# Two orders in the first graph layer: where the scalar engine takes the fourth bank, and where the matrix engine turns the rows

## What is computed

```python
for l in range(3):
    si = x @ attn_w[l, :d]
    sj = x @ attn_w[l, d:]
    scores = si[:, :, None] + sj[:, None, :] + attn_b[l]
    scores = jnp.where(scores >= 0, scores, 0.2 * scores)
    scores = jnp.where(mask, scores, -jnp.inf)
    attn = jax.nn.softmax(scores, axis=-1)
    agg = jnp.einsum('bij,bjd->bid', attn, x)
    h = layernorm(x + agg, g1[l], beta1[l])
    ff = jax.nn.gelu(h @ W1[l] + b1[l], approximate=False) @ W2[l] + b2[l]
    x = layernorm(h + ff, g2[l], beta2[l])
```

## Time and profile before

| | |
|---|---|
| median of three runs | 2901.18 us (2900.43 to 2902.38) |
| profiled execution | 2900.89 us, its span 2899.1 us |
| PE busy over the span | 2633.2 us (91%) |
| DVE | 2045.2 us (71%) |
| ACT | 1928.1 us (67%) |
| POOL | 1674.6 us (58%) |
| first graph layer | about 1304 to 1819 us |
| second and third graph layer | about 1819 to 2780 us |

### The profile page before, as it was taken

How to read it: one execution, slowest core, us unless ns; L and a number is a source line. 1 busy time by engine, 2 the same in 40 slices (tenths; PEclk the granted TensorE clock), 3 DMA queues, 4 the chain that set the end, 5 groups by cost and what they waited for, 6 DMA issues and landing times. The chain is left out here.

```text
span 2899.1 us, 117800 instructions
## 1 busy us (share of the span) xinstructions
PE 2633.2 (91%) x44450; PEld 2409.1 (83%) x44608; DVE 2045.2 (71%) x6167; ACT 1928.1 (67%) x5044; POOL 1674.6 (58%) x2677
## 2 busy tenths in 40 slices
PE   7999999978888888859999999999999999999956
PEld 5777777767777777758999998999999999999945
DVE  6787888844444444448888887777777788888868
ACT  4666666644444444437888887788888778888734
POOL 6777777710000000017888886666666678888845
PEclk9999999999999999979999999999999999999979
DMA  3111111000000000020000001100000100000002
GB/s 90 39 40 39 36 36 36 22 9 13 13 13 13 13 13 13 13 76 25 25 24 25 25 25 39 50 9 9 9 9 9 28 32 9 9 9 9 8 12 105
DMA packets 110837, 74.60 MB, mean 26 GB/s; under 512 B 51504, under 2 KB 109360, under 8 KB 110512
## 3 DMA queue, kind: packets, MB, share of 16 engines
q1 hardware_dynamic: 96800, 61.03, 7.3%
q10 hardware_dynamic: 13968, 12.72, 1.5%
HBM read 51.68 MB, written 22.02 MB: 25 GB/s over the span
## 5 line engine op out<-in xcount | busy, mean ns | idle before, releaser
L1638 PE MATMUL g_H<-g_hT_upper,g_w_upper 128*128 128x256 f32 x1536 | 461.4, 300 | 0.2
L1658 PE MATMUL g_F<-g_w_upper,g_act_upper 128*128 128x256 f32 x1536 | 444.0, 289 | 13.2 <-DVE g_act_rest L1407 12.7
L1638 PE MATMUL g_H<-g_hT_upper,g_w_rest 128*128 128x256 f32 x1536 | 435.1, 283 | 0.0
L1638 PE MATMUL g_H<-g_hT_rest,g_w_upper 128*128 128x256 f32 x1536 | 434.8, 283 | 0.0
L1658 PE MATMUL g_F<-g_w_upper,g_act_rest 128*128 128x256 f32 x1536 | 431.8, 281 | 0.0
L1658 PE MATMUL g_F<-g_w_rest,g_act_upper 128*128 128x256 f32 x1536 | 431.0, 281 | 0.0
L762 POOL COPY l_xt<-seq 128x64 f32 x256 | 60.8, 238 | 598.9 <-PE l_O L773 595.2
L1188 ACT ACTIVATE g_act_raw<-g_H,g_small 128x256 f32<-128x256 f32 x768 | 317.6, 468 | 54.3 <-PE g_H L1638 53.2
L1407 DVE TENSOR_TENSOR g_act_rest<-g_act_raw,g_act_upper 128x512 fp32r<-128x512 f32 x384 | 295.4, 770 | 44.3 <-ACT g_act_upper L1193 37.3
L330 ACT ACTIVATE a_probs<-a_S,a_nmax 128x256 f32<-128x256 f32 x512 | 236.8, 480 | 121.9 <-DVE a_nmax L424 89.0
L1658 PEld LDWEIGHTS g_F<-g_w_upper,g_act_upper 128*128 128x128 f32 x1536 | 289.9, 189 | 23.8 <-DVE g_act_rest L1407 23.6
(11 more groups left out here) (226 smaller groups left out, 8111.3 us busy)
## 6 DMA issues: line engine op xcount, KB each, us to landing
gmask<-masks ACTq DMA_DIRECT2D x97, 128.0 KB, 2.0
x<-in_x_dram SPq DMA_DIRECT2D x32, 256.0 KB, 3.0
a_adj<-in_adj_dram SPq DMA_DIRECT2D x32, 256.0 KB, 2.7
hidden<-l_hs SPq DMA_DIRECT2D x512, 16.0 KB, 1.4
seq<-hidden SPq DMA_DIRECT2D x32, 256.0 KB, 2.7
out_dram<-q_res SPq DMA_DIRECT2D x32, 256.0 KB, 2.1
masks<-gmask SPq DMA_DIRECT2D x32, 128.0 KB, 1.7
g_w_raw<-in_L_gnn_W_dram SPq DMA_DIRECT2D x6, 512.0 KB, 3.8
```

The source lines that it names most:

```text
L1638: last = pe.matmul(hidden_bank[m // 2][:, m % 2 * N:(m % 2 + 1) * N], w[:, c, m * P:(m + 1) * P], x[:, c, :], start=(c == 0 and k == 0), s ...
L1658: last = pe.matmul(ff_bank[:, it * D:(it + 1) * D], x[:, m, it * P:(it + 1) * P], w[:, m, :], start=(m == 0 and it == 0 and k == 0), stop= ...
```

## The change

In the first layer ACT runs `norm1` behind the fourth bank's Gelu and copy, instead of ahead of them. `hT_out` still follows with no table load between. PE runs `turn_h` behind the sixth down chunk, instead of behind the fourth. The layer's last graph and the other two layers keep their order. Line numbers behind the first edit fall by four.

```diff
-                    early = now[0] == 0 and not crossing
-                    feed(*now, range(2, 3))
-                    if early:
-                        norm1(*ahead)
-                    feed(*now, range(3, NB))
+                    feed(*now, range(2, NB))
                     if crossing:
                         w1_uppers(ahead[0], 0)
-                    if early:
+                    if ahead:
+                        norm1(*ahead)
+                    if ahead and now[0] == 0 and not crossing:
                         hT_out(*ahead)
-                    if ahead and not early:
-                        norm1(*ahead)
                     if soon:
                         warm_up(*soon)
-                    if ahead and not early:
+                    if ahead and (now[0] > 0 or crossing):
                         hT_out(*ahead)
@@
-                    turning = 4 if now[0] == 0 and ahead[0] == 0 else 6
-                    down(*now, range(0, turning))
+                    down(*now, range(0, 6))
                     if ahead:
                         turn_h(*ahead)
-                    down(*now, range(turning, MC))
+                    down(*now, range(6, MC))
```

## The result

| | before | after |
|---|---|---|
| median of four runs each | 2901.78 us (2900.43 to 2903.82) | 2958.47 us (2956.07 to 2959.17) |
| profiled execution, span | 2900.89, 2899.1 | 2959.17, 2957.4 |

The changed kernel is slower: ratio 1.0193, 95% interval 1.0176 to 1.0211. The forecast had the sign and the ring (the closed chain of waits from one graph's first Gelu to the next), but 19.6 us for what is 57 us.

The account below looks back on a forecast made before the run. The prediction took a ring of waits between graphs, not matrix work alone, as the bound; loop 20.4 + 0.2, written-out graphs + 2.0 - 3.0 gave 19.6 us more, 2920.5 us, range 2904 to 2934.

Parts of the forecast that it names:

- the ring: First layer's loop: first Gelu, third subtraction, two chunks, turn, hT_out, exponentials, slopes, next Gelu; 16.70 us against 15.85 before.
- the head: Written-out graphs 0 to 2 of the first layer, which still take in a new graph: 0.5 us more each.
- First Gelu to the end of the third subtraction: First step of the ring, ending on DVE, read from the trace before the change: 9.09 us.
- The other terms: Rest of the ring: PE start 0.05, two chunks 1.56, turn 0.77, hT_out to exponentials 2.00, exponentials 1.08, slopes to Gelu 2.15.
- The free half: ACT's reordering: Gelu and copy fit into ACT's existing wait, norm late by 0.1 us at most, fourth copy 2.2 us sooner.
- Graphs 0 to 2: Written-out first graphs, forecast from graph 28's third subtraction and the ring's later steps: 0.5 us more each.
- rival C: Longer PE waits lower its clock, so two chunks and the turn take twice as long: 53 us more, 2973; chance 0.03.
- Graphs 28 to 30: Written-out late graphs: 28 costs 0.5 us more; 29 and 30 take in nothing and gain 1.5 us each.
- Rival A: First layer becomes like the second, the norm's path deciding: 14.85 us per graph, 27 us less, 2874; chance 0.07.
- Rival D: Each ACT table load shows a drain that present waits cover: at most 13 us more, 2933; chance 0.01.

Follow-up runs that it names:

- matrix half alone: Kernel before with only PE's turn moved behind the sixth down chunk, ACT keeping the norm ahead of the fourth bank: 2935.85 us, ratio 1.0122.
- the wait of POOL: Changed kernel, with POOL's addition for the incoming graph waiting until DVE's first subtraction is done: 2934.79 us, ratio 1.0116.
- scalar half alone: Kernel before with only ACT's fourth bank moved ahead of the norm, PE's turn staying behind the fourth down chunk: 2886.93 us, ratio 0.9951.

## Why the prediction was wrong

The sign was right; the size failed in one term of the sum, and in the head.

- *First Gelu to the end of the third subtraction, 9.09 us.* This is the step that failed: 10.44 measured. I had taken it from the kernel before as it stood and bounded only the two instructions at its end, with the reason that POOL's work keeps its place beside DVE. That holds for L1317 (0.69) and for the third subtraction (0.68), neither of which moved. It does not hold at the term's start. My own ring said that DVE would wait for the first Gelu. A wait shifts DVE against everything that does not wait, and POOL's addition was not waiting. Worth 24 x 1.35 = 32 us. The cut of POOL's additions gave 37 us back (27 in the loop), the same cut before the change 7 (4 in the loop), and the wait of POOL moved the slowness from one DVE instruction to the next, to within 0.01 us of what the rows give. Nor was the price right: I had bounded a collision by 1.22 us for a subtraction, with nothing between hit and not hit. The same instruction took 0.69, 0.83, 1.22, 1.67 and 1.82 us in the two kernels, depending on what stood beside it and on how much of that was still to run.
- *The other terms.* 0.05 + 1.56 + 0.77 + 2.00 + 1.08 + 2.15 = 7.61, measured 7.59. The matrix half alone has period 16.91: the forecast 16.70 plus 0.44 on the two-element instruction, less 0.15 on the second subtraction, is 16.99.
- *The free half.* "By ACT alone the edit is free and useful": right for this half alone, a gain of 13 us with a norm that is not late. With the matrix half beside it the gain is gone and the norm is 1.4 us late, by the same collisions.
- *Graphs 0 to 2.* Forecast +1.5, measured +7.1; 2.2 of it is the clock. About 1.0 is the first subtraction of graph 1, 1.67 instead of 0.69 us. Graph 2 has neither, and is still 1.0 us longer where I had put 0.5: its third subtraction ends 9.69 us behind the Gelu before and after, and 9.69 + 7.61 = 17.30 (17.21 measured) against 16.24. I had taken the 0.5 from graph 28, which was already slower before. The rest, most of it in graph 0, I have not split. Of rival C the mechanism was right in two graphs and wrong in the loop, where the clock stays at 1.00 through waits of 1.58 and 1.23 us per graph. Why it falls behind one wait and not behind the next isn't settled: graph 2 waits 1.74 us, as graph 1 does, and keeps 1.00, and with POOL's additions cut it fell behind four of nine equal waits.
- *Graphs 28 to 30.* +0.4 and -3.0, forecast +0.5 and -3.0.
- *Rival A* is the ring of the kernels with the earlier third subtraction, once the norm's real place is put in. In the scalar half alone its sum is 7.69 + 1.15 + 6.00 = 14.84, and 0.44 us that slopes wait for the scores make 15.28; 15.31 is measured.
- *Rival D*: exponentials start 1.40 us after the load's start here too (1526.04 to 1527.44), without a drain.

With 24 x 1.35 = 32.4 for the loop, the forecast's 19.6 becomes 52.0. The 5.6 that the head took above its forecast, which is measured and only in part worked out, makes it 57.6; the span grew by 58.3.

## What to carry to other kernels

When a forecast puts a new wait on one engine, every instruction behind it changes its partner on the engines that don't wait: read again, at the shifted times, which instruction of which engine stands beside each term of the ring, and bound all of them, not only those next to the edit. A term copied from the old trace is good only as far as its neighbours come along. And try the halves of a two-part change apart: here the one was worth 13 us and the other cost 35, and both together cost 57, because the second half took away what the first gained and the collision needs both.

## What the chip showed that I had not expected

- VectorE's subtraction (128 x 512, two operands) started 0.03 us behind a POOL addition ends 0.55 to 0.56 us behind that addition, whether the addition takes 1.29 us (subtraction 1.82) or 0.20 (0.72). The Trainium skill ("SBUF — State Buffer", Who interferes with whom) says that such a pair excludes each other for the whole instruction, and that the order of issue decides who is held up. The rows agree: in the kernel before, the subtraction that started 0.09 us ahead of POOL's power kept its 0.69, and the power took 1.15.
- An instruction on two elements per partition pays too: 0.17 us alone, 0.60 or 0.91 beside one of POOL's additions.
- POOL pays in turn: its power on two elements took 0.69 us at its shortest, and 1.15 to 1.23 beside VectorE's subtraction. Where it stands in front of a norm, that sets a period.
- The granted clock fell to about half behind a wait of 1.83 us in graph 0 and of 1.74 us in graph 1, and not in graph 2 with 1.74 us, nor in 25 graphs with waits of 1.58 and 1.23 us each. In the kernel with POOL's additions cut it fell behind four of nine waits of 1.79 or 1.80 us. So equal waits gave unequal periods.
